# A language-model tower on one core: first items prepared one turn nearer to their use, the passage into the shared expert in another order, the last round of the routed experts in another order

## What is computed

```
h = take(W.T, ids)                         # 16 x 256 tokens, W is 256 x 50257
x = layernorm(h)
for l in range(6):
    y = layernorm(x) * gamma[l] + beta[l]
    q, k, v = split(y @ w_qkv[l], 3)
    q, k = softmax(q, tokens), softmax(k, channels)
    context = einsum('bic,bjc->bij', k, v)
    x = x + einsum('bic,bij->bjc', q, context) @ w_out[l] + b_out[l]
h = h + x
x = layernorm(h)
swiglu = lambda e: (silu(x @ w1[e]) * (x @ w2[e])) @ w3[e]
h = h + swiglu(shared) + sum over the 2 best experts e of prob_e * swiglu(e)
```

## Time and profile before

| | |
|---|---|
| time, median of 3 runs | 1394.66 us (1389.75 to 1396.74) |
| profiled execution, its time | 1381.39 us |
| its span | 1379.6 us |
| PE busy, loading weights | 1235.7 us (90%), 1011.1 |
| DVE, ACT, POOL busy | 1021.6 (74%), 862.5 (63%), 837.1 (61%) |

### The profile page before, as it was taken

How to read it: one execution, slowest core, us unless ns; L and a number is a source line. 1 busy time by engine, 2 the same in 40 slices (tenths; PEclk the granted TensorE clock), 3 DMA queues, 4 the chain that set the end, 5 groups by cost and what they waited for, 6 DMA issues and landing times. The chain is left out here.

```text
span 1379.6 us, 35753 instructions
## 1 busy us (share of the span) xinstructions
PE 1235.7 (90%) x10490; PEld 1011.1 (73%) x10491; DVE 1021.6 (74%) x2668; ACT 862.5 (63%) x2363; POOL 837.1 (61%) x863
## 2 busy tenths in 40 slices
PE   4415889999999999999999999897999999999994
PEld 3314677888888888888888888764565888777773
DVE  2236899999999999999998999885766455555552
ACT  2214678899889988998898788765553233333330
POOL 3057787777677767776787877645754134334443
PEclk8657999999999999999999999998999999999997
DMA  9943655655554554335333675533443465565542
GB/s 338 368 151 92 135 145 130 161 126 134 120 128 97 130 137 101 66 68 117 79 74 61 122 152 91 91 48 93 132 135 122 95 93 86 84 89 89 89 71 32
DMA packets 366103, 161.22 MB, mean 117 GB/s; under 512 B 296880, under 2 KB 350416, under 8 KB 366032
## 3 DMA queue, kind: packets, MB, share of 16 engines
q1 hardware_dynamic: 333200, 121.50, 39.2%
q0 software_dynamic: 19104, 25.32, 10.3%
q10 hardware_dynamic: 13728, 13.63, 2.8%
...
## 5 line engine op out<-in xcount | busy, mean ns | idle before, releaser
L916 PE MATMUL bank<-hT,Wc 128*128 128x256 f16 x2304 | 286.3, 275 | 43.6 <-DMA hT<-hhl 29.2
L916 PEld LDWEIGHTS bank<-hT,Wc 128*128 128x128 f16 x2304 | 226.8, 99 | 71.8 <-issue 44.0
L730 POOL TENSOR_TENSOR h0b<-h0b,rows 128x512 f32<-128x512 f32 x80 | 101.4, 1267 | 137.9 <-DVE h0b L1534 85.8
L844 POOL DMA_INDIRECT out_rows<-h0b,payin x50 | 78.0, 1560 | 128.1 <-DVE h0b L1845 67.2
L916 PE MATMUL bank<-Wc,MT 128*128 128x256 f16 x1152 | 142.7, 274 | 12.7 <-DVE MT L1580 12.7
L916 PE MATMUL bank<-khl,eqT 128*128 128x256 f16 x1152 | 141.3, 272 | 1.5 <-DVE khl L1592 0.3
L916 PE MATMUL bank<-Wc,hT 128*128 128x256 f16 x1152 | 142.1, 273 | 0.0
L1017 PE MATMUL bank<-xTg,Wall 128*128 128x256 f16 x1200 | 136.9, 275 | 3.1 <-DMA payin<-slot_x 3.1
L916 PEld LDWEIGHTS bank<-Wc,MT 128*128 128x128 f16 x1152 | 112.5, 98 | 28.9 <-issue 11.6
L1017 PEld LDWEIGHTS bank<-xTg,Wall 128*128 x1200 | 118.1, 99 | 18.4 <-issue 3.6
L916 PEld LDWEIGHTS bank<-khl,eqT 128*128 128x128 f16 x1152 | 109.5, 97 | 22.7 <-issue 9.2
...
## 6 DMA issues: line engine op xcount, KB each, us to landing
...
```

Source lines behind the costliest of these rows:

```text
L730: pool.tensor_tensor(xn[:, :, :], xn[:, :, :], row(0), ALU.mult).then_inc(s_hg, 1)
L844: pool.indirect_dma_start(out=out_rows, out_offset=bass.IndirectOffsetOnAxis(ap=index, axis=0), in_=source, in_offset=None, compute_op=ALU ...
L916: last = mm(to, lhs(a, k, o), moving, start=(i == 0 and k == 0), stop=(i == 2 and k == 1))
```

## The change

Three parts.

1. **Layer 0.** Statistics of item i move from turn i-7 to i-5, roots with them, `norm` and `first_x` to i-4, POOL's multiply and add to i-4 (now into `hf` both, so that `xn` is free after the multiply), ACT's high half to i-3, SP's `turn_h` to i-3. POOL's gathers stand behind the low half for turns below 0 and between the roots and the low half from turn 0 on. Layer 1 and later stay one turn ahead of that, so turns 11 and 12 hold two items on DVE, POOL and ACT. `HEAD` is 14.
2. **Passage.** PE begins the ups of group 1 between the gates of groups 0 and 1, and the downs of group 0 between those ups. ACT makes the high part of xrow for group g+2 in the middle of group g (before: of g+3 at its start), DVE instead of POOL makes the low part of groups 4 to 7, and POOL's scatters follow each other.
3. **Routed experts.** Payload loads stand before the transposes, tiles have two `gT` buffers, and in the last round the down of pair 23 comes before the ups of pair 24, with DVE's weighing of it ahead of tile 20's low half.

The diff, cut to its core:

```diff
@@ -332,7 +332,7 @@
         AHEAD = 6
 
         PLAIN, CUT, LAST = range(3)
-        HEAD, FIRST_CUT = 12, 3
+        HEAD, FIRST_CUT = 14, 3
...
             def turns(t, p):
-                if have(t + 4):
-                    turn_h(t + 4 if isinstance(t, int) else sp.snap(t + 4), p)
+                if early(t + 3):
+                    turn_h(t + 3, 1 - p)
+                if have(t + 4) and not early(t + 4):
+                    turn_h(t + 4, p)
                 if isinstance(t, int) and t == ITEMS - 3:
...
+                def low_half():
+                    pool.tensor_tensor(hhl[p][:, 1, :, :], hf[:, :, :], hhl[p][:, 0, :, :], ALU.subtract).then_inc(s_h, 1)
+
+                def roots_first():
+                    pool.wait_ge(s_amv, u + 1)
+                    if u >= 2:
+                        pool.wait_ge(s_xn, u - 1)
+                    pool.tensor_scalar(evar[1 - p][:, TB:], amv[1 - p][:, :, 1], EPS, None, ALU.add)
+                    pool.tensor_scalar(evar[1 - p][:, 0:TB], amv[1 - p][:, :, 1], 1.0 + EPS, EPS * EPS, ALU.mult, ALU.add).then_inc(s_avar, 1)
+                    pool.wait_ge(s_avar, u + 1)
+                    pool.tensor_tensor(erstd[1 - p][:, :], evar[1 - p][:, :], mhalf[:, 0:2 * TB], ALU.pow).then_inc(s_arstd, 1)
+
+                if early(t + 4):
+                    pool.wait_ge(s_rows, 48)
+                    pool.wait_ge(s_xn, t + 5)
+                    if t > -4:
+                        pool.wait_ge(s_h, t + 4)
+                    pool.tensor_tensor(hf[:, :, :], xn[:, :, :], row(0, 0), ALU.mult).then_inc(s_hg, 1)
+                    pool.wait_ge(s_hg, t + 5)
+                    pool.tensor_tensor(hf[:, :, :], hf[:, :, :], row(1, 0), ALU.add).then_inc(s_hf, 1)
+                    if early(u):
+                        roots_first()
+                    if t >= 0 and early(t + 7):
+                        gather_item(t + 7)
+                    pool.wait_ge(s_hh, t + 5)
+                    low_half()
+                    if t < 0:
+                        gather_item(t + 7)
+                elif have(t + 4):
                     pool.wait_ge(s_hh, t + 5)
                     pool.sem_inc(s_passed, 1)
-                    low_half(t + 4, p)
-                if early(u):
-                    pool.wait_ge(s_rows, 48)
-                    pool.wait_ge(s_xb, u + 1)
-                    pool.tensor_tensor(xn[:, :, :], xn[:, :, :], row(0), ALU.mult).then_inc(s_hg, 1)
-                    pool.wait_ge(s_hg, u + 1)
-                    if u >= 1:
-                        pool.wait_ge(s_h, u)
-                    pool.tensor_tensor(hf[:, :, :], xn[:, :, :], row(1), ALU.add).then_inc(s_hf, 1)
-                    if t + 8 < NB:
-                        gather_item(t + 8)
-                    if t < -1:
-                        pool.wait_ge(s_hh, u + 1)
-                        low_half(u, 1 - p)
-                elif have(u):
+                    low_half()
+                elif t == -6:
...
             gates_of(0)
+            pe.wait_ge(s_xT[1], 16 * GT)
+            up_shared(1, 0)
             gates_of(1)
-            for g in range(1, NG):
+            down_shared(0)
+            up_shared(1, 1)
+            ranks(0)
+            down_shared(1)
+            ranks(1)
+            up_shared(1, 2)
+            up_shared(1, 3)
+            gates_of(2)
+            for g in range(2, NG):
                 up_shared(g, 0)
-                if g == 1:
-                    ranks(0)
+                if g == 3:
+                    gates_of(4)
                 down_shared(2 * g - 2)
                 up_shared(g, 1)
-                if g == 1:
-                    ranks(1)
+                if g == 2:
+                    ranks(2)
                 down_shared(2 * g - 1)
-                if g == 1:
-                    gates_of(2)
+                if g == 2:
+                    gates_of(3)
                 elif g + 1 < NG:
                     ranks(g + 1)
                 up_shared(g, 2)
-                if g == 1:
-                    ranks(2)
                 up_shared(g, 3)
-                if g + 2 < NG:
+                if g == 2:
+                    ranks(3)
+                elif g + 2 < NG:
                     gates_of(g + 2)
 
 
...
                         up_tile(u, i, e_tile[i + 1], nth_t)
+                        down(j + (SHP - 1), 1 - i, e_pair[i])
                     up_slots(j, i, 0, e_pair[i + 1], nth)
                     if first and i == 0:
                         down_shared(SHP - 2)
                     up_slots(j, i, 1, e_pair[i + 1], nth)
                     if first and i == 0:
                         down_shared(SHP - 1)
-                    else:
+                    elif not last:
                         down(j + (SHP - 1), 1 - i, e_pair[i])
                     if with_tiles:
                         if not last:
                             up_tile(u, i, e_tile[i + 1], nth_t)
                         if not (isinstance(u, int) and u == 0):
-                            down_tile(u - 1 if isinstance(u, int) else pe.snap(u + -1), e_tile[i])
+                            down_tile(u - 1 if isinstance(u, int) else pe.snap(u + -1), 1 - i, e_tile[i])
                     if last:
-                        down_tile(u, e_tile[i + 1])
+                        down_tile(u, i, e_tile[i + 1])
                         down(j + SHP, i, e_pair[i + 1])
...
@@ -1273,14 +1284,16 @@
                     for k in range(TB):
                         last = A(khl[:, 0, k, :], EK[:, k, :], ACT.Copy, scale=rzks[:, k:k + 1])
                     last.then_inc(s_khi, 1)
-                i = t + 5 if isinstance(t, int) and t < -1 else t + 4
-                if have(i) and not (isinstance(t, int) and t == -1):
-                    q = i % 2 if isinstance(i, int) else p
-                    act.wait_ge(s_hf, i + 1)
-                    if not (isinstance(i, int) and i < 2):
-                        act.wait_ge(s_hT[q], landed(i - 2))
+                if early(t + 3):
+                    act.wait_ge(s_hf, t + 4)
+                    if t + 3 >= 2:
+                        act.wait_ge(s_hT[1 - p], landed(t + 1))
+                    A(hhl[1 - p][:, 0, :, :], hf[:, :, :], ACT.Copy).then_inc(s_hh, 1)
+                if have(t + 4) and not early(t + 4):
+                    act.wait_ge(s_hf, t + 5)
+                    act.wait_ge(s_hT[p], landed(t + 2))
                     act.sem_inc(s_passed, 1)
-                    A(hhl[q][:, 0, :, :], hf[:, :, :], ACT.Copy).then_inc(s_hh, 1)
...
-                    normed(3)
-                    high(3)
-                elif g + 3 < NG:
+                if g == 3:
+                    share_exp(4)
+                silu_of(HC * g + 1, 1)
+                high_shared(g, 0)
+                high_shared(g, 1)
+                if g + 2 < NG:
+                    high(g + 2)
+                if g == 2:
+                    share_exp(3)
+                silu_of(HC * g + 2, 0)
+                high_shared(g, 2)
+                silu_of(HC * g + 3, 1)
+                high_shared(g, 3)
+                if g + 3 < NG:
                     normed(g + 3)
-                    high(g + 3)
-                silu_of(HC * g + 1, 1)
-                for c in range(HC):
-                    if g == 1 and c == 2:
-                        share_exp(2)
-                        normed(4)
...
                     stats_of(*late_stats[t])
                 if have(t):
                     dve.wait_ge(s_phi, t + 1)
                     V.scalar_tensor_tensor(PR[:, 1, :, :], p_ps, PS / (KS * WS), PR[:, 0, :, :], ALU.mult, ALU.subtract).then_inc(s_plo, 1)
-                if early(t + 5):
-                    first_x(t + 5, 1 - p)
-                if early(t + 7):
-                    v = t + 7
+                if early(v):
                     dve.wait_ge(s_item[v % 4], 16 * TB * (v // 4 + 1))
                     if v:
                         dve.wait_ge(s_amv, v)
                     for k in range(TB):
                         V.bn_stats(stats[:, k, :], G[:, v * TB + k, :]).then_inc(s_astat, 1)
-                    if not have(u):
+                    if not have(u) or not early(v + 1):
                         first_mean(v, 1 - p)
                 if have(w) and not early(w):
                     dve.wait_ge(s_x, w + 1)
+                    if early(v):
+                        dve.wait_ge(s_amv, v + 1)
...
+            def low(g):
+
+                dve.wait_ge(s_fxhi, g + 1 - EARLY)
+                dve.wait_ge(s_fxlo, g)
+                V.tensor_tensor(xhl(g % ROWS, 1), h0b[:, 1 - g % 2, :, :], xhl(g % ROWS, 0), ALU.subtract).then_inc(s_fxlo, 1)
+
...
+                if g + 2 < NG:
+                    low(g + 2)
                 gate_shared(g, 2)
...
             gated_tile(LEFT - 1)
+            weigh(PAIRS - 2, PAIRS % 2, (PAIRS - 2) % PAYS)
             low_tile(LEFT - 1)
-            gate_and_weigh(PAIRS - 1)
+            gate(SHP + PAIRS - 1, 0)
```

(1 more changed line is left out.)

152 lines of the change are left out of this document (83 added, 69 removed).

## The result

The changed kernel took 1410.64 us (median of 4 runs, 1405.71 to 1415.65) where the kernel before took 1393.41 beside it: a ratio of 1.0132, interval 1.0111 to 1.0152, so **18.4 us slower** (the medians differ by 17.2). The forecast was 1394.6, range 1378 to 1409: the time lies above the range, on the side (slower) that had a chance of 0.29. The profiled execution took 1411.01 us, with a span of 1408.9 (before 1379.6).

What follows compares the result with a forecast made beforehand. TensorE was taken as nearly always busy, so only entry, passage and end could give time back: -10.4 + 12.7 - 2.4 = -0.1 us, with the 13 us difference to the median carried over, 1394.6 us, range 1378 to 1409.

Steps and rivals of the forecast that it cites:

- the side (slower): Whole kernel: the last two rivals, layer 0 not closing at 9.0 us or a slow low half; chance 0.29.
- Entry: Layer 0: 20.3 us gained by turn 10, less 1.5 for lower clock and 8.4 for the hand-over: -10.4 us.
- VectorE's own turn shrinks: Layer 0: X's write falls from 2.28 to 0.86 us away from GpSimd's operations; 0.6 us of it kept.
- The hand-over: Layer 0, turns 11 and 12 holding two items: PE waits some 4.0 us for PR; 8.4 us given back.
- Passage, second half: Shared groups 3 to 5: PE waits 6.3 us each before the gates, slower products cost 8.0; together +26.9 us.
- the gates don't wait: Rival, passage: transposes are there in time and the second half costs nothing; 1368 us, chance 0.10.
- the waits cost no clock: Rival, passage and entry: waits leave the clock up and the hand-over is half hidden; 1381 us, chance 0.20.
- Passage, first half: Up to the down behind group 4's gates: PE has work while VectorE chooses; that down begins 14.2 us sooner.
- End: Output adds: pair 23 is weighed and added sooner, the three behind it follow at old distances; -2.4 us.
- The carried-over difference: Whole kernel: the profiled execution is 13 us below the median of 1394.66, and this was kept in the forecast.
- The sum: Whole kernel: entry -10.4, passage +12.7 and end -2.4 cancel to -0.1 us; chance 0.41.
- The slower rival: Layer 0: the loop doesn't close at 9.0 us a turn; at 9.8 the time is 1403 us, chance 0.24.

Runs made afterwards that it cites:

- e1: The kernel before with only the layer-0 part of the change (HEAD 14): 1376.97 us, 0.9981 of the kernel before.
- e2: The kernel before with only the new order of the passage: 1398.86 us, 1.0143 of the kernel before.
- e6: The changed kernel with the high part of xrow for groups 5 to 7 half a group earlier, the low part following: 1383.95 us, 0.9964 of before.
- e3: The kernel before with only the routed-experts part of the change: 1377.51 us, 0.9989 of the kernel before.
- e5: The full changed kernel measured once more, on another chip: 1411.17 us, 1.0158 of the kernel before.
- e8: The layer-0 part alone, with ScalarE's high half of item 16 and VectorE's norm of item 17 at the end of turn 12: 1383.64 us, 0.9967 of before.
- e7: The layer-0 part alone, with VectorE's eratio moved ahead of the maximum of q: 1386.12 us, 0.9983 of the kernel before.
- e14: The full changed kernel measured a third time, on a chip with slow stretches: 1413.59 us, 1.0135 of the kernel before.
- e13: The kernel before itself, unchanged, run for its trace on a chip with slow stretches: 1395.39 us, 1.0008 of before.

## Why the prediction was wrong, point by point

- **Entry, forecast -10.4, measured -2.6** (e1, -4.4 to -0.7). The first steps held: q of item 0 at 100.43 (100.3), of item 1 at 108.72 (108.4). Then item 4 came at 138.40 instead of 135.4, for which no run gives the cause, and from there q came every 9.5 us on the mean instead of 9.0, so that q of item 12 came at 214.24, not 207.4. The step that failed is "VectorE's own turn shrinks": I took the operation whose neighbour left (X's write) and not the one that moved beside GpSimd's low half (eratio, 0.33 to 1.71 us). The prediction cited the Trainium skill (GPSIMD Engine Reference, "1. Specifications") on just this contention, for the low half of the passage, where it did not come (1.22 us); it came in layer 0, where eratio has two inputs in SBUF. The hand-over cost 10.1 us, from a lead of 13.5 at item 10 to 3.4 at item 14 (forecast 8.4), with PE waiting 4.5 us for PR as said and the next products at a granted clock of 0.51:

```profile
243.13 1.87 PE L964 MATMUL bank<-PR,vT 128*128 128x256 f16 x8 [4.54 <-ACT PR L1318]
...
245.65 2.77 PE L916 MATMUL bank<-khl,eqT 128*128 128x256 f16 x12
```

- **Passage, second half, forecast +26.9**: right in mechanism and nearly in size, +28.3 on the chip of e2 by the forecast's own cut; 27 us back when e6 takes it away. In e2 the three waits are 21.1 us for 18.9, since the transposes took 7.9 us for 6.9, and the slower products 7.2 for 8.0. The rival that "the gates don't wait" is out, and so is the one that the waits cost no clock: behind the three of the changed kernel twelve matmuls took 5.28, 4.07 and 5.12 us for 2.76. The rule of the Trainium skill (TensorE: Matmul & The Clock Gate, "HAM oscillation — how this bites in real kernels") that a wait for a transfer at every tile starts every tile at the lower clock agrees with these rows.
- **Passage, first half, forecast -14.2**: -11.5 by the same cut on a chip without slow stretches (the chain from the second down of group 2 to the gates of group 4 took 15.9 us for 14.7, and e3's own first half is 1.1 shorter than that of the trace of before). On chips with them the gain is gone: 67.3 us in e5 against 66.9 and 69.8 in e8 and e7, and 70.2 in e14 against 69.7 in e13. So nearly all of the 14.2 is missing there (12 to 15 us, by pairs), the largest miss. The waits of rows 6 were taken away from their places as planned; the time went into slow stretches, which the sum did not have and which are longer in the new order than in the old (16 to 19 us in e5 and e14 over the first half of e2, 6 to 9 in e8, e7 and e13 over that of e3).
- **End, forecast -2.4**: -2.1 by the traces, -1.5 in the time. The adds near the end of the changed kernel, the tile's and the pair's:

```profile
1381.99 1.56 POOL L844 DMA_INDIRECT out_rows<-h0b,payt  x1 [3.05 <-issue]
1385.57 1.56 POOL L844 DMA_INDIRECT out_rows<-h0b,payin  x1 [2.02 <-DMA out_rows<-h0b,payt]
```

  3.6 us from the tile's add to the pair's, for 6.9 before and 4.6 forecast. That -2.1 is so near to -2.4 is in part luck: from the tile's add to the last one it is 19.0 us where before has 23.1, so 4.1 less, but the tile's add itself comes 279.2 us after the first routed up where before has 277.2. The sum had nothing for these 2.0 us, and what they hang on was not tested.
- **The carried-over difference.** I added 13 us for the distance of the profiled execution of before to its median, and asked nothing of it. It was the sign of what I missed: the trace of before came from an execution without slow stretches (143.7 us between the landmarks, as on the chips without), and its timed runs of 1390 to 1397 us fit the chips with them (1385 to 1401 us; without, 1375 to 1383). A cost of 8 to 13 us of the kernel before was in the times and not in the trace that I reasoned from, in the very stretch that the change rearranges.
- **The sum.** Without slow stretches the change costs 1.1% (15.6 us) where 0 was forecast: 7.8 of the entry's gain that did not come, 2.7 of the first half's, 0.9 of the end's and 1.4 in the second half; the last 2.9 are the difference between the passage in the traces (16.8) and in the times (19.7), which lies within the interval. With slow stretches it costs 1.3 to 1.6%: in e5 the passage takes 27 us more than in e7 and e8, and entry and end give 4 of them back. On either kind of chip the fault is in the gains far more than in the loss.
- **The slower rival** was that turns of 9.8 us in layer 0 take 8 to 9 us of the gain away. It came nearly true: from m to m the turns took 9.7 us (from q to q 9.5), and 7.8 us of the entry's gain are missing. Its time, 1403, fell short by the passage's first half, of which it said nothing.
